# Four layers of cross-attention and ffn on one core: one ffn's product in three passes, a new order at a seam, and other PSUM banks

## What is computed

```python
x = x + L0_xattn(ln(x), ctx, ...)   # 8 heads, a window of 16 keys
x = x + L0_ffn(ln(x), ...)          # int8 quantised rows: silu(gate) * up, then down
x = x + L1_xattn(ln(x), ctx, ...)   # 32 heads of 128, 8 kv heads
x = x + L1_ffn(ln(x), ...)          # mxfp4 quantised linear layer
x = x + L2_xattn(ln(x), ctx, ctx, ...)   # 32 heads of 16, 8 kv heads
x = x + L2_ffn(ln(x), A, B, Wr)
x = x + L3_xattn(ln(x), ctx, ...)   # 16 heads of 96, 4 kv heads
x = x + L3_ffn(ln(x), ...)          # 3-bit weights, linear layer

def L2_ffn(x, A, B, Wr):            # K = 64 experts of rank 16, the best 16 are used
    scores = xf @ Wr.T
    top_vals, top_idx = top_k(scores, 16)
    G = zeros(N, 64); G[n, top_idx] = softmax(top_vals)
    h = einsum('nd,krd->nkr', xf, A)          # a product 512 x 1024
    return einsum('nkr,kdr->nd', h * G[:, :, None], B) * 2.0
```

## Time and profile before

| | before |
|---|---|
| time, median of 3 runs | 1628.59 us (1627.83 to 1629.03) |
| profiled execution, its own time | 1630.52 us |
| its span | 1628.7 us |
| PE busy | 1546.5 us (95% of the span) |
| DVE busy | 829.4 us (51%) |
| ACT busy | 756.0 us (46%) |
| POOL busy | 519.6 us (32%) |
| the 16 DMA engines, mean | 36 GB/s, 58.05 MB moved |

### The profile page before, as it was taken

The page is one execution under the profiler, slowest core; times in us unless marked ns, Lnnn a source line. Parts: engine busy times, 40 slices in busy tenths (PEclk is TensorE's granted clock), DMA queues, the critical chain, the costliest instruction groups (busy, mean ns, idle before and its releaser), DMA issues. The chain is left out here.

```text
span 1628.7 us, 26021 instructions
## 1 busy us (share of the span) xinstructions
PE 1546.5 (95%) x9538; PEld 1267.0 (78%) x9538; DVE 829.4 (51%) x1703; ACT 756.0 (46%) x2535; POOL 519.6 (32%) x648
## 2 busy tenths in 40 slices
PE   7899998889999999999999998879999999999998
PEld 6777777778889888888988887655555577888876
DVE  4666666464444545554444436676465321343455
ACT  4545545345454554545455455445333211454552
POOL 7667663222222222222222123334222000123423
PEclk9999998999999999999999999999999999999999
DMA  8000001002010100101010110001000001122101
GB/s 246 8 7 8 8 1 40 27 19 79 27 40 27 40 27 1 40 27 40 27 40 27 40 53 1 1 30 53 37 4 0 24 7 48 40 72 74 51 27 62
DMA packets 44414, 58.05 MB, mean 36 GB/s; under 512 B 25472, under 2 KB 32656, under 8 KB 41472
## 3 DMA queue, kind: packets, MB, share of 16 engines
q1 hardware_dynamic: 43872, 56.05, 10.9%
q10 hardware_dynamic: 352, 0.34, 0.1%
q0 software_dynamic: 64, 0.00, 0.0%
HBM read 48.77 MB, written 2.10 MB: 31 GB/s over the span
## 5 line engine op out<-in xcount | busy, mean ns | idle before, releaser
L1801 ACT ACTIVATE big<-pb 128x128 f32<-128x128 f32 x384 | 106.6, 278 | 311.6 <-PE pb L852 202.7
L2165 POOL TENSOR_TENSOR big<-big 128x512 f32<-128x512 f32 x96 | 100.0, 1042 | 260.5 <-DVE big L1442 260.5
L1852 ACT ACTIVATE big<-pb,big 128x128 f32<-128x128 f32 x384 | 136.1, 368 | 64.7 <-issue 41.6
L1437 DVE TENSOR_REDUCE big<-pb 128x4 f32<-128x512 f32 x96 | 65.9, 686 | 181.3 <-PE pb L891 173.7
L867 PE MATMUL pb<-wkh,CXh 128*128 128x256 f32 x512 | 149.0, 291 | 1.5 <-DVE big L1427 1.5
L2155 POOL TENSOR_SCALAR big<-big 128x6 f32<-128x6 f32 x64 | 13.2, 206 | 419.6 <-ACT big L1801 419.3
L867 PE MATMUL pb<-wkl,CXh 128*128 128x256 f32 x512 | 144.3, 282 | 0.0
L867 PE MATMUL pb<-wkh,CXl 128*128 128x256 f32 x512 | 143.6, 280 | 0.0
L1225 DVE TENSOR_TENSOR X<-X,pb 128x512 f32<-128x512 f32 x128 | 87.0, 680 | 96.3 <-PE pb L1073 41.5
L916 PE MATMUL pb<-woh,oh 128*128 128x512 f32 x256 | 111.8, 437 | 8.3 <-DVE X L1225 5.0
L852 PE MATMUL pb<-wqh,CXh 128*128 128x512 f32 x256 | 102.0, 398 | 5.9 <-DVE big L1407 4.5
(11 more groups left out here) (277 smaller groups left out, 3976.3 us busy)
## 6 DMA issues: line engine op xcount, KB each, us to landing
big<-in_w SPq DMA_DIRECT2D x17, 1024.0 KB, 4.9
big<-in_w SPq DMA_DIRECT2D x24, 256.0 KB, 2.9
big<-in_w SPq DMA_DIRECT2D x8, 512.0 KB, 3.5
o<-o SPq DMA_DIRECT2D x96, 32.0 KB, 1.9
X<-in_x SPq DMA_DIRECT2D x8, 256.0 KB, 4.8
big<-in_cn SPq DMA_DIRECT2D x8, 256.0 KB, 2.7
CXlf<-in_cT SPq DMA_DIRECT2D x8, 256.0 KB, 5.2
big<-in_wa SPq DMA_DIRECT2D x1, 2048.0 KB, 7.9
```

The costliest lines, as they stand in the source:

```text
L1437: v.tensor_reduce(m[j % 2], quarters(bank(p)), AX, MAX, negate=True).then_inc(S.m, 1)
L1801: y = a.activation(sq[i % 2], bank(p)[:, j * width:j * width + 128], ACT.Square, accum_out=ss[i % 2][:, first + j:first + j + 1])
L1852: y = a.activation(e_[:, c], bank(p)[:, c], ACT.Exp, bias=m[j % 2][:, k:k + 1], scale=1.0, accum_out=z[j % 2][:, k:k + 1])
L2165: g.tensor_tensor(quarters(e_), quarters(e_), bc(r[j % 2], 128), MUL).then_inc(*on.to(S.pn))
```

## The change

**First layer.** The six f0_split stand two a step in steps 6 to 8, not one a step in steps 7 to 12. The scores of unit 1 go to bank 1. For tiles 0 to 5 the g half of f0_turn goes to bank 0 (was 5), and f0_gate of tiles 0 to 6 to bank 7 (was 6).

**Seam.** l1_begin 0, which splits wq and has SP load, comes behind f0_down 5 and f0_norm 6 and no longer ahead; l1_n 0 comes behind l0_out 30, l0_ctx 30 and l0_weigh 31; l1_k 1 has bank 5 and l1_q 2 bank 7; and the split of the first wo is taken out of l1_k 3 and put behind l1_v 0.

**Third layer's ffn.** f2_h in three passes: 12 F32R matmuls a bank in place of 4 f32. Eight new stages f2_split make the parts of wa, the low part in place of wa itself, two at the end of each of pipe2's steps 3 to 6. f2_turn has ACT copy the transposed rows twice, once whole into a tile of LT that is free then (for f2_a) and once rounded into CXh, and DVE subtract for CXl, which frees the bank. wr lies elsewhere, and SP's l3_begin is now l3_first, one step later, and waits for f2_h 7 as well.

```diff
@@ stage_order
         if step == 4 * NT + 3:
-            together(next(att0), (iter([[("l1_begin", 0)]]), 7), (ffn0, 7), (ffn0, 9))
+            together(next(att0), (ffn0, 7), (iter([[("l1_begin", 0)]]), 7), (ffn0, 9))
-        if 7 <= step < 13:
-            order.append(("f0_split", step - 7))
+        if 6 <= step < 9:
+            order.extend([("f0_split", 2 * step - 12), ("f0_split", 2 * step - 11)])
...
-    for _ in range(3):
+    late = iter(())
+    for step in range(3):
+
         first, second = next(att0), next(att1)
-        together(first[:7], (ffn0, 7))
+        together(first[:7], (late, 6), (ffn0, 7))
+        if step == 0:
+            late = iter([[second.pop(5)]])
         together(second, (ffn0, 1))
...
+        if 3 <= step < 7:
+            order.extend(("f2_split", j) for j in range(2 * step - 6, 2 * step - 4))
...
+        if step == 1:
+            order.append(("l3_first", 0))
@@ psum_uses
     if stage == "l0_scores":
-        return [("S", (0,))]
+        return [("S", (1 if i == 1 else 0,))]
...
     if stage == "f0_turn":
-        return [("g", (5,)), ("u", (3,))] if i < NT - 1 else [("g", (4,)), ("u", (6,))]
+        return [("g", (0 if i < NT - 2 else 5,)), ("u", (3,))] if i < NT - 1 else [("g", (4,)), ("u", (6,))]
...
-    if stage in ("f0_gate", "f0_down") and i < NT - 1:
+    if stage == "f0_down":
         return [("p", (6,))]
...
     if stage == "l1_q":
-        return [("p", (0,))]
+        return [("p", (7 if i == 2 else 0,))]
     if stage == "l1_k":
-        return [("p", (2 if i < 2 else 1,))]
+        return [("p", ((2, 5)[i] if i < 2 else 1,))]
@@ SPLIT
-SPLIT = {k: n for n, k in enumerate((s[:2], i) for s, i in ORDER if s in ("l1_turn", "l3_turn", "f3_turn"))}
+SPLIT = {k: n for n, k in enumerate((s[:2], i) for s, i in ORDER if s in ("l1_turn", "f2_turn", "l3_turn", "f3_turn"))}
...
+        def wa_high(c, n):
+            j = 2 * c + n
+            w, j = (wah0, j) if j < 4 else (wah1, j - 4) if j < 7 else (wah2, 0)
+            return w[:, 512 * j:512 * j + 512]
+
+        def whole_rows(t):
+
+
+            return x_tile(LT, t + 1 if t < NT - 1 else t - 1)
+
+        def f2_parts(j):
+
+            c = slice(512 * j, 512 * j + 512)
+            return wa[:, c], wa_high(j // 2, j % 2), wal[:, c]
@@ tensor_program
                 for c in range(4):
-                    a = pe.matmul(bank(p)[:, 0:64], x_rows(LT, c, t), wr[:, c, :],
-                                  start=(c == 0), stop=(c == 3))
+                    a = pe.matmul(bank(p)[:, 0:64], whole_rows(t)[:, c, :], wr[:, c, :], start=(c == 0), stop=(c == 3))
                 a.then_inc(p.full, 1)
 
             def f2_h(t):
+                on.wait_ge(S.f2l, 8)
                 for n in range(2):
                     p = PSUM["f2_h", t, n]
                     on.wait_ge(p.free, p.n)
-                    for c in range(4):
-                        a = pe.matmul(bank(p), x_rows(LT, c, t), wa[:, c, n * 512:n * 512 + 512],
-                                      start=(c == 0), stop=(c == 3))
+                    k = 0
+                    for x, low in (CXh, False), (CXh, True), (CXl, False):
+                        for c in range(4):
+                            y = wal[:, 1024 * c + 512 * n:1024 * c + 512 * n + 512] if low else wa_high(c, n)
+                            a = pe.matmul(bank(p), x_rows(x, c, t), y, start=(k == 0), stop=(k == 11))
+                            k += 1
                     a.then_inc(p.full, 1)
@@ vector_program
                 on.wait_ge(S.xh, SPLIT[kind, t] + 1)
-                if kind == "l3":
+                if kind == "f2":
                     old = PSUM["l2_s", 2 * t + 1, 1]
...
                 h, t = divmod(i, NT)
                 if t == NT - 1 and h < 7:
                     low_parts(wql, wqh, wq1, 4, S.wqh, S.wql, h + 1)
-                if i == 3:
-                    low_parts(wol, woh, wo1[0], 4, S.woh, S.wol, 0)
...
+                if i == 0:
+                    low_parts(wol, woh, wo1[0], 4, S.woh, S.wol, 0)
...
+            def f2_split(j):
+                x, hi, lo = f2_parts(j)
+                on.wait_ge(S.f2h, j + 1)
+                v.tensor_tensor(lo, x, hi.bitcast(F32), SUB).then_inc(S.f2l, 1)
@@ scalar_program
                 on.wait_ge(p.full, p.n + 1)
                 if user is not None:
                     on.wait_ge(PSUM[user].full, PSUM[user].n + 1)
+                if kind == "f2":
+                    a.copy(whole_rows(t), quarters(bank(p)))
                 if (kind, t) in SPLIT:
                     a.copy(x_tile(CXh, t), quarters(bank(p))).then_inc(S.xh, 1)
                 else:
...
-                if i == 3:
-                    high_parts(woh, wo1[0], 4, D.wo1, 16, S.woh)
...
+                if i == 0:
+                    high_parts(woh, wo1[0], 4, D.wo1, 16, S.woh)
...
+            def f2_split(j):
+                x, hi, _ = f2_parts(j)
+                on.wait_ge(l1_done.full, l1_done.n + 1)
+                on.wait_ge(D.f2, 32)
+                a.copy(hi, x).then_inc(S.f2h, 1)
@@ sync_program
-            def l3_begin(_):
+            def l3_first(_):
                 on.wait_ge(l2_done.full, l2_done.n + 1)
+                read = PSUM["f2_h", 7, 1]
+                on.wait_ge(read.full, read.n + 1)
                 for k in range(3):
                     load_piece(0, k)
```

22 lines of the change are left out of this document (14 added, 8 removed).

## The result

| | before | changed |
|---|---|---|
| median | 1628.21 us (1627.47 to 1629.03, 4 runs) | 1608.88 us (1607.08 to 1611.64, 4 runs) |
| ratio | | 0.9883, 95% interval 0.9866 to 0.9900 |
| profiled execution, its span | 1630.5, 1628.7 us | 1611.6, 1609.8 us |

The prediction was 1607, from 1600 to 1618.

What follows compares the result with a forecast made beforehand. PE, busy 95% of the span, was taken as the bound. The terms -10.6 + 5.5 - 0.5 - 3.5 - 3.3 - 9 = -21.4 us gave 1609.1, set to 1607 us because the median runs 1.9 lower; range 1600 to 1618.

Steps and rivals of the forecast that it cites:

- What bounds: Whole kernel: PE is busy 95% of the span, so only less PE work or a removed PE wait gains time.
- f2_h, -10.6: Third layer's ffn: three F32R passes take 5.6 us a tile instead of 6.93, saving 10.6 us over 8 tiles.
- The covers for the turn and the load: Third layer: other PE work hides f2_turn's extra copy and subtraction and the later l3_first load, costed at nothing.
- Splits, +5.5: Third layer's attention: wa's eight casts and subtractions delay the ACT/DVE loop, costing 5.5 us, range +2 to +9.4.
- The second rival: Half clock in the first layer and GpSimd shutting DVE out at the splits (+10.7): about 1617 us, chance 0.20.
- Start, -0.5: First layer's start: unit 1's scores in bank 1 needn't wait for unit 0's, gaining 0.5 us.
- Tile 0, -3.5: First layer's ffn, tile 0: moving f0_split shortens PE's 3.96 us wait and restores full clock; -3.5 us, range -3 to -4.7.
- Tiles 1 to 5, -3.3: First layer's ffn: new banks for g and gate remove two waits a tile; -3.3 us, range -1 to -5.9.
- My 0.75 a tile: First layer's ffn, tiles 1, 3, 4 and 5: gain per tile if half fall to half clock, between 1.4 and 0.2 us.
- Seam, -9: Between first layer's ffn and next layer: reordering and banks remove PE waits, GpSimd's chain gives some back; -9 us, range -6 to -11.5.

Runs made afterwards that it cites:

- e0: The changed kernel itself, unaltered, measured again: 1607.5 us, ratio to the kernel before 0.9860.
- e1: The kernel before with only the third layer's ffn part of the change (three passes, splits, later load): 1626.9 us, ratio 0.9983.
- e5: The changed kernel with the six f0_split one a step in steps 7 to 12, as before: 1615.2 us, ratio 0.9899.
- e4: The changed kernel with the g half of f0_turn of tiles 0 to 5 back in bank 5: 1607.9 us, ratio 0.9854.
- e6: The changed kernel with the seam's order, banks and wo split as before: 1613.0 us, ratio 0.9888.
- e7: The changed kernel with only the first wo split back in l1_k 3: 1609.4 us, ratio 0.9868.
- e9: The changed kernel with low parts of wa and f0_split a step behind their casts, and wq's casts and low parts earlier: 1602.4 us, ratio 0.9806.
- e3: The changed kernel with DVE's eight low parts of wa one step behind their casts: 1605.6 us, ratio 0.9849.
- e2: The changed kernel without its third layer part, so first layer and seam alone: 1614.1 us, ratio 0.9902.

## Why the prediction was right, and where its steps were not

- **What bounds**: right. The 10.6 us came from PE's work where it is busy throughout, the rest from waits that the list names.
- **f2_h, -10.6**: measured -10.6. The pace of a matmul of the same kind and size elsewhere in the trace was the whole argument, and it held to 0.1 us in each tile. The covers for the turn and the load held too: no wait.
- **Splits, +5.5**: mechanism right, size short, +8.2. The exponentials of units 2 to 5 came 0.7, 3.0, 5.4 and 5.6 us late, almost as I had walked it through, and the loop's period was 8. The step that failed is that nothing is lost once PE takes over as the bound behind unit 5. PE, which had been waiting, ran unit 6 at half clock (L1025 in 2.08 us instead of 1.14) and lost another 2.6 us. In the seven profiles of this order the term was 8.0 to 8.2 in the four with that half clock stretch (the changed kernel, e0, e1, e5), and 5.6 and 7.2, 7.2 in e4, e6 and e7, which run unit 6's scores in 1.14 to 1.37; e6 and e7 fall a little later, in L1004, and lose 1.6 there. The second rival's mechanism for more, GpSimd shutting DVE out, didn't occur here. It occurred at the seam, where I had not looked for it.
- **Start, -0.5**: -0.7. But the new place of f0_split was costed at nothing, and cost 1.7 us between 40 and 60. I had looked at the queue that the splits leave and not at the one that they join, where two casts a step stand ahead of copies that PE waits for.
- **Tile 0, -3.5**: -6.6. I had 2 us for the wait behind L1311 that remains, and it is 1.0; I counted the clock for L798 and L782 and left out the transposes and L769, 1.2 us together; and the gate's own wait of 0.7 us went as well.
- **Tiles 1 to 5, -3.3**: -5.1. A tile at full clock gave -1.9 and not -1.4. (My 0.75 a tile is the mean of 1.4 and 0.2, which is 0.8.) That g's move to bank 0 is needed for the gain was wrong: e4 has 7.7 without it. That some of them fall to half clock was right (clock 0.97 in the stretch, 0.99 before), and such a tile can even lose 1.0.
- **Seam, -9**: -7.3. Up to the wo product my steps held within 1 us: k 0 was 2.1 us earlier (I had 2.8), q 2 7.6 (7.8), q 3 9.1 (8.6), wo 12.2 (11.5), q 4 10.5 (10.4). Then the last transposes gave back 3.2 us where I had 1.5. The wait of q 0 for the low parts, 3.1 us, I had missed; what it cost stays open, as in e9, which doesn't have it, k 0 was 2.9 earlier. The clock at the seam I had put at nothing: where it fell, in e3 and e4, the same order gave -3.0.
- **+1.7 in the third layer**: no step of mine, so put at nothing; the same order, after the same wait, ran at half clock where it had not before. It goes with the place of wo's split, by a way that stays open.

The errors had both signs: 7.8 us of costs missed or short (1.7 + 2.7 + 1.7 + 1.7), 5.3 us of gains (0.2 + 3.1 + 1.8, and 0.2 at the end), and two thirds cancelled. So the time was hit closer than the steps were, and that part is luck.

## What to carry to other kernels

- Where a helper pair is cast on one engine and finished on another, don't put both halves into the same step: give the second half the step after. In the traces that was worth 7.5 us in the third layer and 1.7 in the first, with all the work still there.
- Ask of a moved instruction what stands behind it at its new place as carefully as at its old one; and of a removed wait, which chain is the next latest, to the end of that chain.
- Where PE must stop, several short stops between its work may be safer than a single one of the same sum: with 1.8 us in one piece one to three tiles fell to half clock in each of eight profiles, at a mean clock of 0.97 to 0.98; with 1.0 and 0.7 us only tile 2 did in each of three, behind another wait of 1.9 us, and the stretch kept 0.99. The times of e0 and e4 don't differ for it.

## What the hardware showed that I had not expected

- The clock of TensorE differs from execution to execution at the same wait in the same order: after 1.80 us of idle time tile 1 fell to the lower level in one profile of the changed kernel and not in the next, tile 3 the other way round. A wait of 1.17 us was followed by full clock each time, one of 1.40 us at tile 6 by the lower level in the kernel before, e3, e4, e6 and e7 and by full clock in the changed kernel, e0, e2, e5 and e9. At the seam the same order ran 12 us at a mean of 0.72 (e3, e4) or of 1.00 (e0). A single such fall cost 1.6 to 4.4 us, and the four executions of the changed kernel scatter by 4.6.
- Four DVE subtractions with two SBUF inputs took 2.50, 3.34 or 4.41 us, as GpSimd had no operation, one, or two and the tail of a third beside them, and GpSimd's operations grew from 1.16 to 1.47 and from 1.05 to 1.44.
